# An expert layer on one core: the first layer and its biases reordered, and scaled high parts moved to ScalarE

## The reference

```python
# L0, for each batch: u = v = fside[b] (128 x 16)
z1 = einsum('bfi,bir->bfr', x, v) / 128
z = einsum('bfr,bor->bfo', z1, u) / 16
L0 = gelu(einsum('bfi,oi->bfo', x, W) + fc_bias + z + b, exact)
# L1: gate scores w_be from segment means of x and from cond, best 2 of 4 experts
out = 0
for e in range(4):
    h = gelu_tanh(x @ ew1[e] + eb1[e])          # 128 -> 512
    out += w_be[:, e] * mask[e] * (h @ ew2[e] + eb2[e])   # 512 -> 128
L1 = out + gelu_tanh(x @ sw1 + sb1) @ sw2 + sb2
```

## Time and profile before

| | us |
|---|---|
| median of 3 runs (lowest, highest) | 277.92 (275.48, 278.88) |
| the profiled execution, its time | 276.94 |
| its span, first to last instruction | 274.8 |
| TensorE busy | 244.4 (89%) |
| VectorE busy | 198.8 (72%) |
| ScalarE busy | 156.2 (57%) |
| GpSimd busy | 22.2 (8%) |

### The profile page before, as it was taken

One profiled execution on the slowest core, in us unless ns is written; L12 is line 12 of the kernel. 1 busy time (PEld: TensorE's weight loads), 2 busy tenths in 40 slices (PEclk: granted clock), 3 DMA queues, 4 the chain that ended last, 5 costly groups with the idle time before them and its releaser, 6 DMA issues.

```text
span 274.8 us, 3451 instructions
## 1 busy us (share of the span) xinstructions
PE 244.4 (89%) x1217; PEld 203.2 (74%) x1217; DVE 198.8 (72%) x441; ACT 156.2 (57%) x286; POOL 22.2 (8%) x39
## 2 busy tenths in 40 slices
PE   8964969799979997999989997999979989999963
PEld 7763748678768875888768885887768959898852
DVE  0266799999369565797399795797499959779661
ACT  4375799630894439760894439751835194544400
POOL 5000000940000000000000060000000600000000
PEclk9995598999999999999999999999999999999987
DMA  6995000000001000010001000010001000100101
GB/s 129 235 284 96 1 1 0 0 2 0 0 2 38 0 0 4 6 32 2 1 0 38 2 0 0 6 36 0 0 0 41 0 0 0 43 0 0 38 0 38
DMA packets 15811, 7.40 MB, mean 27 GB/s; under 512 B 6175, under 2 KB 14515, under 8 KB 15795
## 3 DMA queue, kind: packets, MB, share of 16 engines
q1 hardware_dynamic: 14781, 6.98, 10.6%
q10 hardware_dynamic: 854, 0.18, 0.3%
q0 software_dynamic: 160, 0.02, 0.1%
HBM read 5.09 MB, written 2.10 MB: 26 GB/s over the span
## 4 chain that ended last, share of the span: by engine, by line
PE 61%; ACT 16%; DVE 14%; issue 4%; DMA 2%; SPq 2%; DVEq 0%; ACTq 0%
PE ps L449 19%; PE ps L451 17%; PE ps L450 17%; ACT h L373 5%; ACT hs_hi L376 4%; DVE hs_lo L700 4%; DVE hs_hi L695 3%; PE ps L496 2%; DMA x_tok<-in_x 2%; DVE W_lo L679 2%; ACT L373 2%; ACT L354 2%; PE ps L508 2%; DVE hs_lo L689 2%; ACT W_raw L359 2%
## 5 line engine op out<-in xcount | busy, mean ns | idle before, releaser
L373 ACT ACTIVATE h<-ps,b_col 128x512 f32<-128x512 f32 (+1 forms) x160 | 94.1, 649 | 60.5 <-PE ps L451 38.4
L700 DVE SCALAR_TENSOR_TENSOR hs_lo<-h,w_be,hs_hi 128x512 fp32r<-128x512 f32 (+1 forms) x128 | 78.4, 673 | 0.0
L449 PE MATMUL ps<-x_hi,W_hi 128*128 128x512 f32 (+1 forms) x160 | 65.1, 407 | 14.2 <-ACT h L373 5.5
L449 PE MATMUL ps<-hs_hi,W_hi 128*128 128x512 f32 (+1 forms) x160 | 59.9, 375 | 6.3 <-DVE hs_lo L700 4.9
L695 DVE TENSOR_SCALAR hs_hi<-h,w_be 128x512 fp32r<-128x512 f32 (+1 forms) x128 | 50.3, 455 | 13.7 <-ACT h L373 6.9
L451 PE MATMUL ps<-x_lo,W_hi 128*128 128x512 f32 (+1 forms) x160 | 60.0, 375 | 0.0
L450 PE MATMUL ps<-x_hi,W_lo 128*128 128x512 f32 (+1 forms) x160 | 59.8, 374 | 0.0
L451 PE MATMUL ps<-hs_lo,W_hi 128*128 128x512 f32 (+1 forms) x160 | 59.0, 369 | 0.0
L450 PE MATMUL ps<-hs_hi,W_lo 128*128 128x512 f32 (+1 forms) x160 | 59.0, 369 | 0.0
L449 PEld LDWEIGHTS ps<-x_hi,W_hi 128*128 128x128 f32 x160 | 30.8, 192 | 27.9 <-ACT hs_hi L376 10.8
L449 PEld LDWEIGHTS ps<-hs_hi,W_hi 128*128 128x128 f32 x160 | 30.6, 191 | 11.6 <-DVE hs_lo L700 2.8
(11 more groups left out here) (102 smaller groups left out, 173.4 us busy)
## 6 DMA issues: line engine op xcount, KB each, us to landing
W_raw<-in_L_cond_ew SPq DMA_DIRECT2D x8, 256.0 KB, 4.9
out<-x_tok SPq DMA_DIRECT2D x8, 256.0 KB, 2.3
x_tok<-in_x SPq DMA_DIRECT2D x6, 168.0 KB
x_tok<-in_x SPq DMA_DIRECT2D x3, 176.0 KB
W_raw<-in_L_cond_sw SPq DMA_DIRECT2D x2, 256.0 KB, 5.0
x_tok<-in_x SPq DMA_DIRECT2D x3, 84.0 KB
F_raw<-in_fside_Bx1x1024x SPq DMA_DIRECT2D x3, 64.0 KB, 5.3
x_tok<-in_x SPq DMA_DIRECT2D x2, 88.0 KB
```

The lines of the kernel that those rows point to most:

```text
L373: ins = nc.scalar.activation(span(h[:, k % 3, c, :], s), up_bank(k, c), ACT.Gelu_apprx_tanh, bias=b1_col[:, s, c:c + 1])
L449: nc.tensor.matmul(dst, w_hi, m_hi, start=start, stop=False)
L700: nc.vector.scalar_tensor_tensor(hs_lo[:, k % 2, :, c], h[:, k % 3, :, c], w_be[:, t * NB + b, s - 1:s], f32(hs_hi[:, k % 2, :, c]), ALU.m ...
```

## The change

It has four parts.

1. **Start.** VectorE's block of segment sums and time gate moves from behind the first low part of x (t = 1) to behind the next (t = 2), with the first low weight in it; `output_rows` and `modulation` move behind `gate_in`, and the low weights 1 and 2 ahead of `gate_logits`. TensorE does the product for the modulation behind `up(0)` and the logits behind `up(1)`.
2. **Biases.** GpSimd waits for each tile t until `split(f - 2)` is done before it adds the biases.
3. **Late first layer.** `matrices` and `layer0` move one place earlier, to before and behind `down(f + 1)`, and so do `matrix`, `gelu0_late`, `residual`, the segment sums and the high and low parts of x.
4. **High parts.** For steps 3, 4 and 5 (`HI_ON_ACT`) ScalarE makes `hs_hi` by four scaled copies of h behind the step's gelu; VectorE makes `hs_lo` alone.

```diff
+    HI_ON_ACT = [3, 4, 5]
...
             for t in range(NT):
+
+                pool.wait_ge(lo_ok, parts_until(first_step(t) - 2))
                 pool.wait_ge(bias2_ok, next(g for g, (a, z) in enumerate(GATES) if a <= t < z) + 1)
...
+            def scaled_high(k):
+                t, s = STEPS[k]
+                a, z = SPAN[s]
+                act.wait_ge(h_ok, CH * (k + 1))
+                act.wait_ge(w_ok, 1)
+                act.wait_ge(down_ok, k - 1)
+                for b in range(NB):
+                    c = slice(b * L + a, b * L + z)
+                    nc.scalar.activation(hs_hi[:, k % 2, :, c], h[:, k % 3, :, c], ACT.Copy,
+                                         scale=w_be[:, t * NB + b, s - 1:s]).then_inc(act_hi_ok, 1)
...
             for k in range(2, K):
                 gelu(k)
+                if k in HI_ON_ACT:
+                    scaled_high(k)
...
-                t = late_tile(k, 4)
+                t = late_tile(k, 3)
                 if t is not None:
                     gelu0_late(t)
-                t = late_tile(k, 6)
+                t = late_tile(k, 5)
                 if t is not None:
                     x1_high(t)
...
+            up(0)
             pe.wait_ge(eb2T_read, NSEG)
             pe.wait_ge(mod_terms_ok, 1)
             nc.tensor.matmul(psMod, ones[:, :], mod_terms[:, :, :], start=True, stop=True).then_inc(mod_ps, 1)
-            up(0)
+            up(1)
             logits(0)
-            up(1)
             for k in range(K):
...
                     transpose_F(t)
+                t = late_tile(k, 1)
+                if t is not None:
+                    matrices(t)
                 down(k)
+                t = late_tile(k, 0)
                 if t is not None:
                     xT(t)
                 t = late_tile(k, 1)
-                if t is not None:
-                    matrices(t)
-                t = late_tile(k, 2)
                 if t is not None:
                     layer0(t)
...
+                if k in HI_ON_ACT:
+                    for b in range(NB):
+                        c = slice(b * L + a, b * L + z)
+                        dve.wait_ge(act_hi_ok, NB * HI_ON_ACT.index(k) + b + 1)
+                        nc.vector.scalar_tensor_tensor(hs_lo[:, k % 2, :, c], h[:, k % 3, :, c],
+                                                       w_be[:, t * NB + b, s - 1:s], f32(hs_hi[:, k % 2, :, c]),
+                                                       ALU.mult, ALU.subtract).then_inc(lo_ok, 1)
+                    return
...
-                t = late_tile(k, 2)
+                t = late_tile(k, 1)
                 if t is not None:
                     matrix(t)
-                t = late_tile(k, 4)
+                t = late_tile(k, 3)
                 if t is not None:
                     residual(t)
```

More of the change, by code:

```diff
@@ L156, in build @@
         up_ps, h_ok, hi_ok, lo_ok, down_ok = sem("up_ps"), sem("h_ok"), sem("hi_ok"), sem("lo_ok"), sem("down_ok")
+        act_hi_ok = sem("act_hi_ok")
         outT_ok, out_ps, out_tok_ok, out_left = sem("outT_ok"), sem("out_ps"), sem("out_tok_ok"), sem("out_left")
@@ L598, in _ @@
                 layer0(t)
-                if t == 1:
+                if t == 2:
                     pe.wait_ge(bias_in, 16 * 3)
                     nc.tensor.transpose(psEb2T, eb2_raw[:, :], ident[0:E, 0:E]).then_inc(eb2T_ps, 1)
+            up(0)
             pe.wait_ge(eb2T_read, NSEG)
@@ L691, in split @@
                     return
-                before_k = sum(NB for j in range(k) if STEPS[j][1] > 0)
+                if k in HI_ON_ACT:
[6 more added lines that the diff above has]
+                    return
+                before_k = sum(NB for j in range(k) if STEPS[j][1] > 0 and j not in HI_ON_ACT)
                 for b in range(NB):
@@ L827, in _ @@
                     x1_low(t - 1)
-                if t == 1:
+                if t == 2:
                     segment_sums(0, 2)
+                    weight_low(WEIGHTS[0])
                     time_gate()
-                    output_rows()
-            weight_low(WEIGHTS[0])
             segment_sums(2, 4)
             gate_in(0)
+            output_rows()
+            x1_low(NA - 1)
             dve.wait_ge(bias_in, 16 * 3)
             modulation()
-            x1_low(NA - 1)
-            gate_logits(0)
             weight_low(WEIGHTS[1])
             weight_low(WEIGHTS[2])
+            gate_logits(0)
             split(0)
@@ L855, in _ @@
                     weight_low(WEIGHTS[2 * k + 3])
-                t = late_tile(k, 2)
+                t = late_tile(k, 1)
                 if t is not None:
                     matrix(t)
-                t = late_tile(k, 4)
+                t = late_tile(k, 3)
                 if t is not None:
                     residual(t)
-                t = late_tile(k, 5)
+                t = late_tile(k, 4)
                 if t is not None and t % 2 == 1:
                     segment_sums(t - 1, t + 1)
-                t = late_tile(k, 6)
+                t = late_tile(k, 5)
                 if t is not None:
```

## The result

The changed kernel takes 281.0 us (median of 4 runs, 280.08 to 282.0) against 278.06 of the kernel before measured with it: ratio 1.0148, 95% interval 1.0104 to 1.0191. It is slower by 1.5%, less than the 2% that count as a difference here, and the median is where the forecast put it. The profiled execution took 282.0 (span 280.3) against 276.94. By the ratio the change costs 4.1 us (2.9 to 5.3), by the two medians alone 2.9. The ratios leave out executions that lie over 1.5% above the fastest of their kernel (one of e2's six, four of e4's twelve, two of e9's and three of e11's twelve), so that a kernel with a wide scatter comes out a little low.

The account below looks back on a forecast made before the run. TensorE's work plus its gaps was taken to bound the kernel, with VectorE setting the pace until 55.6. Terms -3.4 + 2.6 + 0.6 + 0.5 + 3.7 = +4.0 on 276.94 gave 281.0 us, range 276.0 to 285.0.

Parts of the forecast that it names:

- the waits: All terms but the clock's, from the start to the late tiles: together +0.3 us.
- The lead: Start to end of split(2): earlier logits 0.6, low weights 1.6, less GpSimd interference 1.2; 3.4 us gained, 52.0 instead of 55.44.
- the lower bound of 1.8: Smallest gain at the end of split(2), if the logits come as late as before and half the interference stays.
- The wait at the transposes: Behind down(2), TensorE's transposes for tile 4 wait for four scaled copies and the factor's copy on ScalarE: +2.6 us.
- High parts by ScalarE worth 0 to VectorE's side: Steps 3 to 5: freeing VectorE of 12 instructions gains 0, since TensorE no longer waits for VectorE behind step 2.
- That step 5's copies cost nothing: Step 5's four scaled copies on ScalarE run while TensorE has 5.5 us of other work.
- The late first layer: Tiles 4 to 7: second table load follows T, the end of down(f+2); gap 2.2 for 1.5, four times +0.15, +0.6 us.
- Counted from the end of the matrices, the split ends at 4.0: VectorE in late tiles: the late matrix delays split(f+2), which still ends before down(f+2) asks for it at 5.5.
- Gate weights of tile 7: VectorE's 2.1 us of gate weights make the split end at 6.1 against 5.5 asked for: +0.5 us (0 to 1.0).
- The clock: Behind five new TensorE gaps over 2 us, the granted clock falls about three times: +3.7 us (0 to 7.8).
- the one without falls: Rival: the clock holds in the new gaps, the sum is +0.3, time 277.3 us; chance 0.22.
- That the load drains: Rival: each late-tile table load costs 1.4 us more, gaps of 3.6 us make a fall sure, 288 us; chance 0.02.

Follow-up runs that it names:

- e2: Kernel before with only the late first layer moved one place earlier (old start, no GpSimd wait, high parts on VectorE): 280.59 us, ratio 1.0132.
- e4: Changed kernel with ScalarE's copy of the transposed factor moved ahead of step 4's scaled high parts: 278.12 us, ratio 1.0002 to the kernel before.
- e9: Changed kernel with the tanh table loaded early, behind the detour's gelu, and the output sum ahead of the late gates' logits: 275.82 us, ratio 0.9931 to the kernel before.
- e11: Kernel before with only GpSimd's bias additions waiting tile by tile for a split: 276.14 us, ratio 0.9939.
- e1: Kernel before with only the reordered start and GpSimd's wait for a split: 274.49 us, ratio 0.9911.
- e8: Changed kernel with factor's copy first, early table load and output sum first, high parts kept on ScalarE: 270.03 us, ratio 0.9706 to the kernel before.
- e7: Changed kernel with early table load and output sum first, and all high parts back on VectorE: 268.55 us, ratio 0.9660 to the kernel before.
- e3: Kernel before with only the high parts of steps 3 to 5 made by ScalarE: 282.47 us, ratio 1.0196.
- e5: Changed kernel with the tanh table loaded by a one-column activation right behind the detour's gelu: 278.49 us, ratio 1.0045 to the kernel before.
- e6: Changed kernel with VectorE's output sum ahead of the gate's logits at both late gates: 281.62 us, ratio 1.0127 to the kernel before.
- e10: Changed kernel with extra unread products keeping TensorE at work in its new gaps: 281.34 us, ratio 1.0139 to the kernel before.

## Why the prediction came out right

By its number it was right; by its steps, errors cancel, and that it came out at 281.0 exactly is luck. It had +0.3 for the waits and +3.7 for the clock. The profile has more of the first and less of the second. The sum itself, +4.0, was put on a profiled execution of 276.94, which lies 1.1 under the median of 278.06; the measured difference is 4.1 by the ratio, 2.9 by the medians and 5.1 between the two profiled executions.

**The lead** (3.4): the mechanism was right, the size too large. e1's own profile has 3.64 at down(2), e11 has 1.1 from GpSimd's interference against 1.2. But the means over all profiles are 2.1 apart, and e1 is faster by 2.5. The rows that the working started from show a late execution: its clock was low from 19.7 to 33.4, and down(2) starts at 55.59, at 54.27 in e2, with the same start, where the clock was low from 20.6 to 30.8. The changed kernel's own profile shows 1.5, under the lower bound of 1.8, because of the late transfer of x and the clock's fall at 12 us, which no step dealt with. It came in four of the nine profiles with the new start; whether the new start makes it more likely, no run shows.

**The wait at the transposes** (2.6): right, 2.74. In e4 it goes with the one copy moved. Four scaled copies of 344 columns took 2.00 where 1.9 was taken from the gelus of the same width.

**High parts by ScalarE worth 0 to VectorE's side**: right, as far as e8 against e7 can tell. That step 5's copies cost nothing was not quite right: with the load repaired, they hold the first detour by 0.9 (gap 1.66 for 0.71).

**The late first layer** (0.15 per tile): the mechanism was right, the gap 1.99 for 2.2, a tile 0.34 longer (31.14 for 30.80): 1.4 for four, where 0.6 was said.

**The third tile's 1.40**: this is the step that failed. "Counted from the end of the matrices, the split ends at 4.0" looks at splits alone. Of down(f+4) the prediction says nothing, and its wait for the out sum, `outT_ok`, which is in the code of `down`, has no term in the sum: the cost was put at nothing without a reason. The out sum behind the late gate's logits was on the path as soon as everything ahead of it was later. With the predicted lead the waits now add up to -3.4 (lead) + 2.74 (transposes) + 1.4 (third tile) + 0.26 (gate weights) + 1.4 (four detours) = +2.4, where the prediction had +0.3; this term is two thirds of the difference.

**Gate weights of tile 7** (0.5): 0.26. The fourth tile took 0.90 more than before: 0.34, 0.26, and 0.3 that the rows give no wait for. (Some of it is the reading: matmuls overlap, so each new gap delays what follows by some 0.16 more than its bracket says.)

**The clock** (3.7, from three falls in five gaps): too much in number. Its count of "two of three gaps over 2 us" leaves out two of the five in its trace: 3.99 ahead of 22.54, in which the clock fell at 19.7, and 2.68 ahead of 28.12, with the clock still low. In the changed kernel's profile two falls stand behind new gaps, at the transposes and in the first tile. What they cost was as predicted: from the transposes to the product behind the first T 16.47, against 14.88 in e4 (55.45 to 70.33), 1.6 where 1.4 was said; behind T 0.6 (76.31 to 87.66 against 10.71), and over the kernels between 0.5 and 1.2, where 1.1 was said. Together 2.2. In the 16 gaps of 1.99 of four profiles there are eight falls: half, not two thirds, and not evenly. Behind the first tile's gap the clock fell in all four, behind the other twelve four times. Behind the gap of 2.74 it fell in all five profiles that have one.

The profile's first 4.0 us are so: -1.5 lead, +2.74 and 0.16 more for the overlap of the matmuls ahead of that gap (e3, e5 and e6 have the same 5.73 or 5.74 from down(2) to the transposes, 2.83 without the gap), +1.6 and +0.6 for the two falls, +0.36 left for the detour. The timed parts do not add up so well: -2.5, +3.7 and +5.4 make +6.6 (error some 2 us), the whole is +4.1 (error 1.2). The difference of 2.5 is about what the error allows, so the times neither show nor refute that the parts add.

Of the rivals, the one without falls would have been 276.94 + 2.4 = 279.3, not 277.3. That the load drains is refuted in each of the four tiles, as in the first: 1.28 at 73.69 and the next activation at 74.99. The Trainium skill (ScalarE: Activation LUTs, What ACT_TABLE_LOAD costs) has 1.38 more for each switch; no run here shows it.

## What to carry to other kernels

For every instruction that the change makes later, read all its waits and all who wait for it: the forecast missed a bank's hand-over that stood in plain code, just above the wait that it had read. Work given to the idler engine stands in that engine's queue ahead of something; here four short copies cost 2.74 us and the relief brought nothing that could be measured, and with the hand-over ahead of them that wait is gone. Compare several profiles before a lead is read off one: the start of this kernel moves by 1.3 us between executions of the same order. A table load stands where its first user stands; issue an activation of one column of the next function ahead of the wait, and the load is paid in the wait.

## What the runs showed of the hardware

The same gap is not always followed by a fall of the granted clock: behind gaps of 2.74 us it fell in five of five, behind 1.99 in eight of sixteen, behind 1.66 to 1.67 in one of three (e8), behind 1.31 in one of four (e10). In the start it fell while TensorE was busy with small products (1.00 us busy of 1.00 at 0.50), in just the four profiles in which a transfer of x had held TensorE for 0.57 to 0.94 us shortly before. One fall cost 0.5 to 1.6 us: least where the products behind it waited for gelus anyway.

GpSimd and VectorE slow each other: an addition of 168 columns took 783 ns beside split(2) (2.35 for three, e11), and 443 in the later tiles (1.33 for three, e11); the 24 of the changed kernel took 559 on average against 789 in the kernel before, where 12 stood in one piece beside the splits; a low part of 512 columns 0.68 instead of 0.90.
